# The late tiles' table by step sums in three parts, the last rows' gate values written earlier, and the early table behind chunk 27

## The reference

```python
logits = xf @ gate_w + gate_b
one_hot = jax.nn.one_hot(jnp.argmax(logits, axis=-1), E, dtype=xf.dtype)
h = jax.nn.gelu(jnp.einsum('td,edh->teh', xf, w1), approximate=True)
y = jnp.einsum('teh,ehd->ted', h, w2)
out = jnp.einsum('te,ted->td', one_hot, y)
```

## Time and profile before

| | us |
|---|---|
| median of 3 runs (range) | 722.25 (722.22 to 722.46) |
| profiled execution, its own time | 728.13 |
| its span, first to last instruction | 726.0 |
| PE busy in the span | 641.2 |
| DVE busy in the span | 614.9 |

### The profile page before, as it was taken

One profiled execution on the slowest core, in us unless ns is written; L12 is line 12 of the kernel. 1 busy time (PEld: TensorE's weight loads), 2 busy tenths in 40 slices (PEclk: granted clock), 3 DMA queues, 4 the chain that ended last, 5 costly groups with the idle time before them and its releaser, 6 DMA issues.

```text
span 726.0 us, 16639 instructions
## 1 busy us (share of the span) xinstructions
PE 641.2 (88%) x5448; PEld 334.7 (46%) x5448; DVE 614.9 (85%) x1568; ACT 494.1 (68%) x1007; POOL 412.9 (57%) x929
## 2 busy tenths in 40 slices
PE   5498789889887798899999999999999998868994
PEld 2276567666655322222333332333333222868994
DVE  6868999998977998899999999999999984655552
ACT  3534556766645348888888888888898888524662
POOL 4112566575556447217576787878778736353553
PEclk9789999999999859999999999999999999988998
DMA  6564142353262222036330301203030002356410
GB/s 184 139 245 126 45 132 81 96 175 108 83 205 89 87 77 99 1 96 180 92 88 2 111 23 50 73 13 110 24 100 24 24 34 70 107 160 173 126 32 12
DMA packets 42340, 67.05 MB, mean 92 GB/s; under 512 B 7964, under 2 KB 35583, under 8 KB 39056
## 3 DMA queue, kind: packets, MB, share of 16 engines
q1 hardware_dynamic: 38480, 56.73, 26.3%
q0 software_dynamic: 3296, 8.41, 3.2%
q10 hardware_dynamic: 480, 0.85, 0.5%
HBM read 43.22 MB, written 23.04 MB: 91 GB/s over the span
## 4 chain that ended last, share of the span: by engine, by line
PE 44%; DVE 31%; ACT 11%; issue 6%; POOL 2%; DMA 2%; SPq 1%; another core or an unknown queue 1%; ACTq 0%; POOLq 0%; DVEq 0%
DVE arena L1544 19%; PE bank L1055 8%; ACT arena L1955 5%; PE pair L1044 5%; PE pair L1306 5%; PE bank L1016 4%; DVE arena L1377 3%; PE bank L1315 3%; PE pair L1315 2%; DVE arena L1406 2%; PE bank L901 2%; ACT arena L1924 2%; PE bank L912 2%; PE bank L886 2%; POOL arena L629 1%
## 5 line engine op out<-in xcount | busy, mean ns | idle before, releaser
L1955 ACT ACTIVATE arena<-pair 128x512 f32<-128x512 f32 x506 | 278.2, 603 | 52.0 <-PE pair L1044 49.7
L1544 DVE TENSOR_REDUCE arena<-bank 128x1 f32<-128x512 f32 x388 | 251.6, 683 | 7.1 <-PE bank L1016 6.1
L1044 PE MATMUL pair<-q_stack,k_stack 64*128 64x512 bf16 x506 | 158.8, 386 | 6.2 <-ACT arena L1955 5.0
L1016 PE MATMUL bank<-k_stack,q_stack 63*128 63x512 bf16 x388 | 137.4, 395 | 8.8 <-DVE arena L1544 5.0
L1055 PE MATMUL bank<-arena,values 128*9 128x512 f32 x1024 | 134.4, 597 | 2.1 <-ACT arena L1955 1.5
L1377 DVE TENSOR_TENSOR arena<-bank,cst 128x512 f32<-128x512 f32 x128 | 82.2, 684 | 16.2 <-PE bank L886 15.6
L1544 DVE TENSOR_REDUCE arena<-pair 128x1 f32<-128x512 f32 x124 | 84.5, 681 | 1.5 <-PE pair L1016 1.1
L1016 PEld LDWEIGHTS bank<-k_stack,q_stack 63*128 63x128 bf16 x388 | 33.2, 93 | 109.6 <-DVE arena L1544 25.0
L694 POOL TENSOR_TENSOR arena<-arena 128x32 f32<-128x32 f32 (+6 forms) x312 | 68.4, 219 | 24.4
L1044 PEld LDWEIGHTS pair<-q_stack,k_stack 64*128 64x128 bf16 x506 | 40.6, 93 | 49.3 <-ACT arena L1955 25.2
L2096 ACT ACTIVATE fq_all<-pair 128x512 f32<-128x512 f32 x39 | 23.3, 596 | 42.1 <-PE pair L1306 27.7
(11 more groups left out here) (301 smaller groups left out, 1269.6 us busy)
## 6 DMA issues: line engine op xcount, KB each, us to landing
linear_parts<-arena SPq DMA_DIRECT2D x8, 768.0 KB, 3.7
q_stack<-linear_parts SPq DMA_DIRECT2D x48, 128.0 KB
softmax_parts<-arena SPq DMA_DIRECT2D x8, 768.0 KB
q_stack<-softmax_parts SPq DMA_DIRECT2D x48, 128.0 KB
k_stack<-softmax_parts SPq DMA_DIRECT2D x48, 128.0 KB
k_stack<-linear_parts SPq DMA_DIRECT2D x42, 128.0 KB
arena<-in_L_ffn_w_dram SPq DMA_DIRECT2D x16, 256.0 KB, 4.6
v_all<-token_rows SPq DMA_DIRECT2D x20, 192.5 KB, 2.6
```

Source lines behind the costliest of these rows:

```text
L1016: pe.matmul(bank[:], qs[b % 2][rows, slot, qt * P:(qt + 1) * P], ks[b % 2][rows, slot, :], start=True, stop=True).then_inc(d_s_m, 1)
L1044: pe.matmul(score_bank(s)[:], ks[u][rows, 2 * g + x, kt * P:(kt + 1) * P], qs[u][rows, 2 * g + x, :], start=True, stop=True).then_inc(d_s_ ...
L1544: dve.reduce_max(mx[:, m % 2, col:col + 1], bank[:], AX).then_inc(d_s_mr, 1)
L1955: act.activation(pt[:, kt % 2, x, half, :], score_bank(s)[:], ACT.Exp, scale=SCALE).then_inc(d_s_e, 1)
```

## The change

The late table is cut into three parts. Part 0 (counts to the scan) stands behind `placed(B-1)`, part 1 behind `tile_steps(7)`, part 2 behind `tile_steps(8)`. A tile's start is no longer a masked sum over all 8 experts of 22 by 8 values, but the first expert's value plus a sum of 7 steps between neighbouring experts. The masks `mine`, `head` and the minimum over the whole array go. The early table is computed in the same way, all three parts in one place, behind `d_normalise(27)` (n = 31, kt = 1) in place of behind `add(26)` (n = 30, kt = 3). In the last rows two copies (gb and the token numbers) go to a new function `end_rows_ready` between `turned_out(1)` and `turned_out(2)`; `turned_out(2)` now stands before the last `add` and `end_stats(1)`; and the rest of `end_rows` stands behind `turned_out(3)`.

```diff
-                    made_one(dve.tensor_tensor(mine, by_tile(index), k.rep(base[:], n), ALU.is_ge))
-                    made_one(dve.tensor_tensor(mine, mine, tail, ALU.subtract))
-                    made_one(dve.tensor_tensor(head, by_tile(k.cst[:, C_STARTS:C_STARTS + n]), k.rep(shifted[:], n), ALU.add))
-                    made_one(dve.tensor_tensor(tail, head, k.rep(limit[:], n), ALU.min))
-                    made_one(dve.tensor_tensor(head, head, tail, ALU.subtract))
-                    made_one(dve.tensor_tensor(tail, tail, mine, ALU.mult))
-                    made_one(dve.reduce_sum(offset[:, at], tail, AX))
-                    dve.tensor_copy(k.offset_i[:, at], offset[:, at]).then_inc(d_s_ta, 1)
-                    made_one(dve.tensor_tensor(head, head, mine, ALU.mult))
-                    made_one(dve.reduce_sum(expert[:, at], head, AX))
...
+                        made_one(dve.tensor_tensor(limit_step[:, 0:NE - 1], limit[:, 1:NE], limit[:, 0:NE - 1], ALU.subtract))
...
+                        made_one(dve.tensor_tensor(shift_step[:, 0:NE - 1], shifted[:, 1:NE], shifted[:, 0:NE - 1], ALU.subtract))
...
+                        made_one(dve.tensor_tensor(steps, behind[:, :, 0:NE - 1], k.rep(shift_step[:, 0:NE - 1], n), ALU.mult))
+                        if late:
+                            rooms = room_of[:, 0:n, 0:NE - 1]
+                            made_one(dve.tensor_tensor(rooms, behind[:, :, 0:NE - 1], k.rep(limit_step[:, 0:NE - 1], n), ALU.mult))
...
+                        made_one(dve.reduce_sum(begin[:, at], steps, AX))
+                        if late:
+                            made_one(dve.reduce_sum(last_row[:, at], rooms, AX))
+                        all_made()
+                        made_one(dve.scalar_tensor_tensor(begin[:, at], begin[:, at], shifted[:, 0:1],
+                                                          k.cst[:, C_STARTS:C_STARTS + n], ALU.add, ALU.add))
...
+                        made_one(dve.scalar_tensor_tensor(offset[:, at], last_row[:, at], limit[:, 0:1], begin[:, at],
+                                                          ALU.add, ALU.min))
                         all_made()
                         dve.tensor_copy(k.offset_i[:, at], offset[:, at]).then_inc(d_s_ta, 1)
...
+                def end_rows_ready():
+
+                    rows, gb = rows_high[:, 0:C], k.rep(k.gb_all[:, (B - 1) * D:B * D], C)
+                    for f in range(END, T):
+                        wait(dve, k.s_rs[(f + 6) % SLOTS], stored((f + 6) % SLOTS, f))
+                    dve.tensor_copy(rows[:, :, D:2 * D], gb).then_inc(d_s_xe, 1)
+                    dve.tensor_copy(rows[:, :, 3 * D:ROW], k.ids[:, END:T].unsqueeze(2)).then_inc(d_s_xe, 1)
...
-                        if kt == 3 and n == NB - 2:
+                        if kt == 1 and n == NB - 1:
...
                 turned_out(0)
                 turned_out(1)
+                end_rows_ready()
+                turned_out(2)
                 dve.wait_ge(d_s_fp, T)
...
                 end_stats(1)
-                turned_out(2)
-                tile_steps(1)
+                turned_out(3)
+                end_rows()
+                result(0)
                 end_logits(0, ring[2])
...
                 tile_steps(4)
-                end_rows()
                 end_logits(1, ring[0])
...
                 tile_steps(6)
                 placed(B - 1)
+                total = ring[2][:, P + C * NE:P + C * NE + NE]
+                table(True, total, 0)
                 tile_steps(7)
-                table(True, ring[2][:, P + C * NE:P + C * NE + NE])
-                for j in range(8, MT):
+                table(True, total, 1)
+                tile_steps(8)
+                table(True, total, 2)
+                for j in range(9, MT):
                     tile_steps(j)
```

More of the change, by code:

```diff
@@ L315, in program @@
         taken, spent = d([NE]), d([NE])
-        over, past, own, begin = d([NE, T]), d([MT - NA, NE]), d([MT - NA, NE]), d([MT - NA, NE])
-        expert, offset = d([MT]), d([MT])
+        over, past, own, room_of = d([NE, T]), d([MT - NA, NE]), d([MT - NA, NE]), d([MT - NA, NE])
+        expert, offset, begin, last_row = d([MT]), d([MT]), d([MT]), d([MT])
+        shift_step, limit_step = d([NE]), d([NE])
         h = k.h_tiles
@@ L1609, in all_made, with table @@
                     dve.wait_ge(d_s_tb, made[0])
-                def table(late, total):
+                def table(late, total, part):
                     j0, n = (NA, MT - NA) if late else (0, NA)
@@ L1617, in table @@
                     at = slice(j0, j0 + n)
[L1618 to L1627, removed]
-                        all_made()
@@ L1658, in table @@
-                    all_made()
-                    made_one(dve.tensor_tensor(head, by_tile(k.cst[:, C_STARTS:C_STARTS + n]), k.rep(shifted[:], n), ALU.add))
-                    made_one(dve.tensor_copy(k.expert_i[:, at], expert[:, at]))
-                    all_made()
-                    if not late:
-                        made_one(dve.tensor_tensor(head, head, mine, ALU.mult))
-                        made_one(dve.memset(k.drop[:, at], 0.0))
-                        all_made()
-                        made_one(dve.reduce_sum(offset[:, at], head, AX))
+                    behind = past[:, 0:n]
@@ L1689, in end_rows @@
                     dve.wait_ge(d_s_fb, T)
-                    for f in range(END, T):
-                        wait(dve, k.s_rs[(f + 6) % SLOTS], stored((f + 6) % SLOTS, f))
+                    dve.wait_ge(d_s_fh, END + 1)
                     dve.tensor_tensor(d_on[:], h[:, END:T, 0:D], gb, ALU.mult).then_inc(d_s_xe, 1)
-                    dve.tensor_copy(rows[:, :, D:2 * D], gb).then_inc(d_s_xe, 1)
-                    dve.tensor_copy(rows[:, :, 3 * D:ROW], k.ids[:, END:T].unsqueeze(2)).then_inc(d_s_xe, 1)
                     dve.wait_ge(d_s_xe, 3)
@@ L1788, in _ @@
                             add(n - G, ring_bank(n, kt, 4))
-                        if kt == 3 and n == NB - 2:
+                        if kt == 1 and n == NB - 1:
                             at = dispatch_at(EARLY - 1) + C * NE
                             dve.wait_ge(d_s_fe, C * EARLY + 3)
-                            table(False, d_ot[:, 2, at:at + NE])
+                            for part in range(3):
+                                table(False, d_ot[:, 2, at:at + NE], part)
                 def end_stats(i):
```

82 lines of the change are left out of this document (48 added, 34 removed).

## The result

The changed kernel takes 715.69 us (median of 4, 713.35 to 716.12), the kernel before 722.36 beside it (4 runs, 722.22 to 724.43). The ratio is 0.9887, 95% interval 0.987 to 0.9904: 6.7 us less by the medians. The profiled execution took 713.35, its span is 711.2; that of before had 728.13 and 726.0.

The account below looks back on a forecast made before the run. Once the tiles run, PE bounds the kernel: each us it loses before 661.8 lengthens the end. Terms -1.1 - 1.1 - 2.3 - 2.9 + 0.3 = -7.1 take 722.25 to 715.1 us, range 710.5 to 720.8.

Parts of the forecast that it names:

- Start and last rows: PE's gaps at tile 3 and its wait at tile 8 before the last counts: -1.1 us each.
- Late table: Three parts between tiles behind the counts: PE loses 2.9 us where it lost 5.2, so -2.3 us.
- Clock behind the table: PE behind the late table: longest hole about 1.4 us, so no half-clock spell, -2.9 us.
- Early table: New place behind d_normalise(27): takes 4.3 us, to 613.5, and delays the start by +0.3 us (bounds 0 and +1.4).
- SP's first load: First tile load, not hidden behind the early table: issued about 614.7, landed 617.3, against the turn at 617.21.
- The profile's own hole: PE's 3.37 us idle at 640.12, with its slow spell 6.2 us, taken to explain the profile's 5.88 us surplus.
- the model of the ordinary run: Trace of the kernel before without the hole at 640.12 and its slow spell; last counts at 639.6.
- A: Rival, behind the counts: the clock still drops once, the 2.9 us stay, 718.0 us; chance 0.14.
- D: Rival, behind the counts: three holes bring three half-clock spells, each costing 3.4 us, 725.4 us; chance 0.06.
- clock 1.00 from 617: Sign in the new trace: PE at full clock from 617 to the end of the tiles.
- Rival C: The hole at 640 is real and the new order removes it: 6.2 us go as well, 708.9; chance 0.06.
- rival B: PE's signals are held up in every run, so moving the late table closes no hole: 720.4 us; chance 0.11.

Follow-up runs that it names:

- the turn of tile 2 first alone: Kernel before with only turned_out(2) moved ahead of the last add and end_stats(1), and turned_out(3), result(0) behind them: 717.64 us, ratio 0.9936.
- second trace of before: The kernel before, unchanged, run again beside other runs of itself: 732.1 us against 729.62, ratio 1.0019.
- the three parts alone: Kernel before with only the late table in three parts by step sums; early table, turns and last rows in old places: 731.01 us, ratio 1.0018.
- the third group: Four kernels run on one chip beside the kernel before, unchanged, which took 729.62 us there against 721.81 and 722.57 in the other two groups.
- the filled hole: Changed kernel with the late table in one piece again, plus 18 unread fp32 matmuls in PE's hole: 717.21 us, ratio 0.993.
- the one-piece kernel: Changed kernel with the late table in one piece again behind tile_steps(7), in the new arithmetic: 719.2 us, ratio 0.9964.
- second trace of the changed kernel: The changed kernel run again, nothing altered: 715.31 us, ratio 0.9899 of the kernel before.
- the one with the early table back: Changed kernel with only the early table back in its old place (n = 30, kt = 3): 711.97 us, ratio 0.9856.
- the filled start: Changed kernel with 10 unread fp32 matmuls in PE's hole before it turns chunks 28 to 31: 713.69 us, ratio 0.9877.

## Why the prediction was right, and where it was not

The forecast was 715.1, the result 715.69: faster by 6.7 us for 7.1. By its terms:

*Start and last rows*, forecast -2.2. The chain from the chunks' turns to the counts takes 20.97 us in the changed kernel (615.00 to 635.97), against 23.5 modelled for before: -2.5. With the turn of tile 2 first alone it was 21.65, so 1.85 come from the start and 0.7 from the last rows. Tile 5's new gap is 0.40 for 0.9. What the term lacked is the clock: the two gaps of 2 us in sum bring a half-clock spell that costs 3.2 us in some executions (seen in the second trace of before and in that of the three parts alone, absent in the first trace of before, from which the forecast was made). The kernel with the turn of tile 2 first measured -4.9 and has no such gaps. That the ordinary runs of before had the spell mostly is argued from this, not traced: both traces that have it are of the third group.

*Late table*, forecast -2.3 for the holes: 2.9 us lost where I had 2.9, and the parts took 1.68, 1.55 and 2.28 for 1.7, 1.5 and 2.2. Right, in sum and in parts; the distribution over the tiles was different.

*Clock behind the table*, forecast -2.9: by the filled hole 2.0. The spell can be 3.4 us long (649.0 to 652.4 in the one-piece kernel, and 3.4 in the second trace of before) or 6.8 as in the earlier trace rows and in the kernel with tile 2 first; the forecast took the long one for every execution. The 2.0 are of the one-piece kernel; before itself was not run with its hole filled. With the holes the one-piece kernel should cost 4.0 more than the changed one, and cost 3.9.

*Early table*, forecast +0.3 with bounds to +1.4: wrong, +3.3. The step that failed is the sentence that ACT's `weights(0)` "holds up the numerators' copy 0.1". Three things made it false, and the traces give each its size. I had the table 4.3 us long and it took 5.56 there (4.4 in the old place): 1.26. I gave a register read behind the signal to SP and none to ACT, where `weights(0)` begins 0.96 us behind the cast; with the cast's end at 613.5 and the 0.53 from `weights(0)` to the copy, that alone makes the copy some 0.3 late against the 614.70 of the trace before. And in the trace of before, one of late signals, PE's last values come at 613.58, in the changed kernel's at 611.28, 2.30 sooner, while the table starts only 1.98 sooner (607.22 for my 609.2): 0.3. Together 1.9, and PE's gap is 2.67 for 0.81. SP's first load, for which I feared, was issued at 613.88 and held nobody up. And I gave the gap no price in clock; filling it gave 1.6 back.

*The profile's own hole.* The reason was wrong: a whole group of runs has it, with times to match, and nothing ties it to profiling. And that its 6.2 us match the surplus of 5.88 is in part luck. 1.6 of the surplus had come in before the tiles, as said above, so some 4.3 are left for them. Taking out 6.2 leaves the model of the ordinary run about 2 us too short there (an estimate, as the first 582 us differ by 2.6 us from trace to trace), and the spell at tile 3, which that trace lacks, is of this size. That two sizes matched was no proof of where the surplus lay.

The sum by what was measured: -2.5, -2.3, -2.0, +3.3 give -3.5, and the spell at the start -3.1: -6.6, beside the 6.7. Two terms off by 3 us each cancelled, so that the forecast came within 0.6 us of the result is luck; of its mechanism the chain at the start and the late table's place held. Rivals A and D asked for half clock behind the counts: none in the changed kernel's traces. A spell before them, at 615, was in neither. I had written clock 1.00 from 617, and that half clock anywhere there in an ordinary run would show the prediction wrong. The second trace of the changed kernel has it until 621.76, and so have four more kernels with that gap: by its own sign this part of the prediction is wrong. Rival C's hole is real, as it said, but by their times the runs compared did not have it. Where it stands, in the third group, the three parts alone gained nothing, as rival B has it.

## What to carry to other kernels

Work of several us on an engine with spare time should lie in pieces between the tiles; 2 of the 3.9 us that it saved here were the clock of TensorE behind the hole. When a producer is moved later, look in each consumer's order for what stands behind its wait: the cost was not the waiting step but the copy queued behind it, and the register read behind the late signal adds to it. Before a model is built on one trace, compare its own time with the median; the surplus is a condition of that execution, and the slack read from it may not exist in the others. If one hole seems to explain the surplus, check with a second trace that the stages before the hole have none of it.

## What the runs showed of the hardware

- A gap on PE of 2 to 2.5 us, alone or in two pieces, is followed by half clock in most executions and not in all: in five of six traces at the chunks' turns (four times for 6.8 us at a cost of 1.8 to 2.0, once for 3.4 at 0.9) and in two of three at tile 3 (6.8 us, at 3.2 in one of them). Behind the gap of 0.81 in the same place no trace has it. The kernels with such a gap scatter: before 719.43 to 725.06 in 23 runs, the changed one 714.05 to 716.46 in 6; the one with the early table back 711.52 to 712.41 in 5.
- The spells behind the table's hole of 4.2 to 5.1 us were 6.8 us long in two traces and 3.4 in two.
- Matmuls whose result nobody reads, put in a hole of 4.3 us, kept the clock at 1.00 and made the kernel 2.0 us faster; twice as many made it 1.0 slower.
- In the third group signals of PE reach DVE and ACT 3 us and more late (DVE idle 2.92 us until 642.40, though PE's turn of that tile stands at 637.54), and the kernel before took about 1% longer (729.62 for 721.81 and 722.57). POOL issues indirect DMAs back to back there, six from 635.19 to 642.54. They don't make it by themselves: the kernel with tile 2 first has six as close (626.86 to 634.20) and no late signal. What makes it is open.
- ACT's `weights(0)` began 0.96 us behind the end of the cast that it waited for, in three traces (612.78 to 613.74, 613.78 to 614.74, and with the filled start).
